# Fused attention and 4-bit FFN on eight cores: softmax scaling moved from VectorE to GpSimd, odd score blocks copied out of PSUM by VectorE

## What is computed

```python
def _mhsa(X, ln_g, ln_b, Wq, bq, Wk, bk, Wv, bv, Wo, bo):
    Xn = (X - mu) * rsqrt(var + EPS) * ln_g + ln_b
    Q, K, V = split_heads(Xn @ Wq + bq), ...         # 16 heads of 128
    scores = einsum('bhqd,bhkd->bhqk', Q, K) / sqrt(128)
    scores = where(causal, scores, -inf)
    A = softmax(scores, axis=-1)
    AV = einsum('bhqk,bhkd->bhqd', A, V)
    return AV @ Wo + bo

x = layernorm(x + attention(x))
# FFN: gate, up (16384 x 2048) and down (2048 x 16384), 4-bit values
# with one scale per 32, dequantised on the chip
x = layernorm(x + (gelu(x @ Wg.T) * (x @ Wu.T)) @ Wd.T)
```

## Time and profile before

| what | us |
|---|---|
| the kernel before, median of 2 runs | 12190.67 |
| lowest and highest of them | 11885.47, 12495.87 |
| the profiled execution, its own time | 11891.69 |
| its span, slowest core (core 7) | 11890.1 |
| spans of the eight cores | 11810.8 to 11890.1 |
| busy in the span: PE, DVE, ACT, POOL | 7283.3, 3800.4, 2362.9, 952.1 |

### The profile page before, as it was taken

The page is one execution under the profiler, slowest core; times in us unless marked ns, Lnnn a source line. Parts: engine busy times, 40 slices in busy tenths (PEclk is TensorE's granted clock), DMA queues, the critical chain, the costliest instruction groups (busy, mean ns, idle before and its releaser), DMA issues.

```text
span 11890.1 us, 99736 instructions; the slowest of 8 cores (11810.8 to 11890.1 us)
## 1 busy us (share of the span) xinstructions
PE 7283.3 (61%) x31488; PEld 3182.4 (27%) x31488; DVE 3800.4 (32%) x8321; ACT 2362.9 (20%) x3461; POOL 952.1 (8%) x1531
## 2 busy tenths in 40 slices
PE   3473341332232233777777777777756999999993
PEld 1131120111111011333233332332322444444441
DVE  1103221221221212555555555555541111221122
ACT  1213323232222112222222222222221000000001
POOL 0010000000000000111111111111100000000000
PEclk9785565556556566888888888888878999999996
DMA  5572333224324236666666666666642222222222
GB/s 82 78 91 46 48 53 65 42 45 63 47 38 61 39 36 108 115 115 111 111 111 112 113 116 112 113 111 110 111 93 92 73 76 78 75 78 71 82 72 74
DMA packets 1927393, 971.47 MB, mean 82 GB/s; under 512 B 1762928, under 2 KB 1832656, under 8 KB 1885920
## 3 DMA queue, kind: packets, MB, share of 16 engines
q0 software_dynamic: 530400, 415.45, 22.1%
q1 hardware_dynamic: 1396480, 549.66, 21.0%
HBM read 667.01 MB, written 218.10 MB: 74 GB/s over the span
## 4 chain that ended last, share of the span: by engine, by line
PE 46%; DMA 23%; DVE 13%; ACT 9%; issue 6%; SPq 2%; DVEq 0%; POOL 0%; ACTq 0%; POOLq 0%
PE pp L793 24%; PE pp L842 12%; DMA regC<-regD 8%; DMA regC<-regC 3%; PE pp L386 3%; DMA regC<-usc 3%; DVE regD L664 3%; DMA regD<-regD 3%; PE pp L288 2%; ACT regD L638 2%; PE pp L425 2%; DVE regD L497 2%; DMA regD<-wo 2%; DMA wspd<-regD 2%; PE pp L544 2%
## 5 line engine op out<-in xcount | busy, mean ns | idle before, releaser
L793 PE MATMUL pp<-regB,regC 128*128 128x512 bf16 x16384 | 3705.9, 390 | 978.8 <-ACT regC L810 603.7
L793 PEld LDWEIGHTS pp<-regB,regC 128*128 128x128 bf16 x16384 | 1635.5, 100 | 3044.3 <-issue 1215.2
L842 PE MATMUL pp<-regC,regD 128*128 128x512 bf16 x8192 | 1986.7, 406 | 528.0 <-DMA wspd<-regD 373.1
L842 PEld LDWEIGHTS pp<-regC,regD 128*128 128x128 bf16 x8192 | 833.2, 103 | 1681.4 <-issue 871.9
L425 PE MATMUL pp<-regC,regB 128*128 128x128 bf16 x2176 | 272.7, 307 | 1622.2 <-DMA regC<-regD 829.4
L815 DVE TENSOR_TENSOR regC<-regC,pp 128x512 bf16<-128x512 bf16 x512 | 328.4, 683 | 2553.7 <-PE pp L793 2553.1
L664 DVE TENSOR_TENSOR regD<-regD,regC 128x512 bf16<-128x512 bf16 (+1 forms) x1024 | 948.7, 957 | 196.2 <-ACT regD L638 179.8
L872 DVE TENSOR_TENSOR regA<-pp,regA 128x512 f32<-128x512 f32 x960 | 658.6, 690 | 1062.0 <-PE pp L842 1061.7
L638 ACT ACTIVATE regD<-regD 128x1024 bf16<-128x1024 fp8e4 (+1 forms) x512 | 432.0, 844 | 2619.2 <-DVE regD L634 2496.9
L810 ACT ACTIVATE regC<-pp 128x512 bf16<-128x512 f32 x512 | 276.6, 592 | 3063.2 <-PE pp L793 3063.2
L386 PE MATMUL pp<-regC,regD 128*128 128x512 bf16 x1024 | 351.2, 518 | 671.3 <-DVE regC L363 671.3
(11 more groups left out here) (81 smaller groups left out, 4123.9 us busy)
## 6 DMA issues: line engine op xcount, KB each, us to landing
wspg<-regC SPq DMA_DIRECT2D x128, 1024.0 KB, 4.6
regC<-wspg POOLq DMA_DIRECT2D x128, 1024.0 KB, 5.3
wspd<-regD SPq DMA_DIRECT2D x128, 512.0 KB, 3.1
regD<-wspd POOLq DMA_DIRECT2D x128, 512.0 KB, 3.9
regD<-x POOLq DMA_DIRECT2D x48, 1024.0 KB, 7.6
regD<-wq POOLq DMA_DIRECT2D x64, 512.0 KB, 6.5
regD<-wo POOLq DMA_DIRECT2D x64, 512.0 KB, 7.0
regD<-wv POOLq DMA_DIRECT2D x32, 512.0 KB, 8.0
```

What stands on the lines that cost most here:

```text
L793: e.matmul(out=pp[b][:], lhsT=WGT[:, w, k, p:256:2], rhs=H1T[:, k, tt * 1024 + t * 512: tt * 1024 + (t + 1) * 512], start=(k == 0), stop=( ...
L842: b=db, w=wd: e.matmul(out=pp[b][:], lhsT=WDT[:, p, 4 * w + c, p2:256:2], rhs=INTER[:, 2 * c + p, t * 512: (t + 1) * 512], start=(c == 0 a ...
```

## The change

Two edits, and the bookkeeping for a semaphore that POOL's computing instructions count up.

1. In `emit_tail` the scaling of the row by the reciprocal (line 408) is issued on POOL and not on DVE. It keeps its place in the Python code, so it goes into POOL's list where that list stands at the time. The transpose waits for POOL.
2. For full key blocks with odd `ks` (below the diagonal block), DVE and not ACT copies and scales the 512 scores from PSUM, followed at once by their maximum. Such a block exists once per tile in groups 3 and 2 (`ks` = 1), and not in groups 1 and 0.

```diff
-SEMS = ENGS[:3] + DMASEMS
+SEMS = ENGS[:3] + ("pool",) + DMASEMS
...
-                        ev_an = E("dve", lambda e, kl=klen_, ar=ar_, pa=par_:
+                        ev_an = E("pool", lambda e, kl=klen_, ar=ar_,
+                                  pa=par_:
                             e.tensor_scalar(
                                 out=ar[:, 0:kl], in0=ar[:, 0:kl],
                                 scalar1=stat(S_RCP + 4 * pa), scalar2=None,
...
-                            waits=mw({"dve": ev_an}, ev_atb_free[par_]),
+                            waits=mw({"pool": ev_an}, ev_atb_free[par_]),
...
                             if ks < g:
+                                if ks % 2 == 1:
+                                    eve = E("dve", lambda e, b=sb, k=ks,
+                                            ww=w, sr=srow: e.tensor_scalar(
+                                            out=sr[:, k * 512:k * 512 + ww],
+                                            in0=pp[b][:, 0:ww],
+                                            scalar1=ISQ, scalar2=None,
+                                            op0=OP.mult),
+                                        waits=mw({"pe": evs},
+                                                 ev_srow_free[par]))
+                                    ev_psum_free[sb] = {"dve": eve}
+                                    ev_cm = E("dve", lambda e, k=ks, ww=w,
+                                              sr=srow: e.tensor_reduce(
+                                            out=stat(S_CM0 + k),
+                                            in_=sr[:, k * 512:k * 512 + ww],
+                                            axis=AX, op=OP.max),
+                                        waits={"dve": eve})
+                                    ev_last_S = evs
+                                    continue
...
-        CSEMS = ("pe", "act", "dve")
+        CSEMS = ("pe", "act", "dve", "pool")
```

## The result

The changed kernel takes 13430.16 us (median of 12 runs, lowest 12878.88), the kernel before 12380.54 (median of 10, lowest 11885.47). In many executions of every kernel here the cores of one die or both ran at a lower clock and took longer: over the executions without that the ratio is 1.084, 95% interval 1.066 to 1.102, and where an experiment had few or none of them (e1, e2, e4, e6, e11) it is compared by cores 4 to 7 or by the heads of core 7 alone. The changed kernel is slower, as forecast, but by more: I had 12515 us with 12210 to 12950 for an execution like the profiled one, 5.2% over it.

The account below looks back on a forecast made before the run. The prediction took a serial ring of waits through the engines, none near full, as the bound. It added 340 + 51 + 133 + 15 + 86 = 625 us to 11891.7, forecasting 12515 us, range 12210 to 12950.

Parts of the forecast that it names:

- The ring: Per tile: DVE scaling, transpose, PE matmuls, ACT copy, DVE maxima run serially, 10.91 us a turn; additions paid in full, 256 times.
- POOL's time per scaling: Edit 1: POOL takes 1.83 us per row against DVE's 0.50, extra 1.33 us x 256 = 340 us.
- that row: DVE's line 573, the nearest plain operation: 2292 ns for 2048 columns, 1.12 ns a column, 1.22 us for the mean row.
- the sum of 625: Whole program: 340 scaling + 51 delay + 133 Wq panels + 15 Wo + 86 edit 2, in us.
- My bounds, 0 and 1150 us: POOL's scaling: from DVE's 0.50 us, extra 0, to ACT's slowest 4.59 ns a column, extra 4.49 us per row.
- POOL's delay: Edit 1: POOL reacts later to a semaphore, between 0 and 0.46 us; taken as 0.2 us x 256 = 51 us.
- The late panels: Wq panels now behind tile 2's scaling land late in every group, net 133 us; first Wo panels add about 15.
- the 193: Projections of heads 1 to 15 wait for late Wq panels, mean 3.2 us x 60 = 193 us.
- the 60 that come back: Tile 3's transposes no longer meet the panel: 3 us in group 0, 1 in group 1, x 15 = 60 back.
- Wo's 15: Two first Wo panels also stand behind the last scaling: 4 us on each of four groups, about 15.
- Edit 2: DVE's score copy lengthens tiles by 0.60 us in group 3, 0.74 in group 2: 86 us, between 45 and 105.
- much slower: Rival: POOL's scaling takes three times line 573, 3.66 us, extra 809 us, time 12985 us; chance 0.20.

Follow-up runs that it names:

- e1: Changed kernel without edit 2 (scaling on POOL, odd score block left on ACT): lowest of 6 runs 13135.68 us; heads 856 us above the kernel before.
- e2: Kernel before with edit 2 alone (DVE copies the odd score block): lowest of 6 runs 12353.70 us; heads 88 us more than before.
- e4: Kernel before, each Wq panel also waiting for tile 2's scaling of the head before, on DVE: lowest of 6 runs 12482.89 us; heads 182 us more.
- e6: Edit 1 alone, row scaled as float32 pairs by immediate 1.0, half the columns, division left out: one run, 13001.07 us; heads 3016.1 us.
- e11: As e4, but the panel waits for tile 2's reciprocal instead of its scaling: lowest of 3 runs 12664.81 us; heads 2732.5 us.
- e5: Edit 1 alone with immediate 1.0 in place of the reciprocal from memory, division left out: lowest of 3 runs 12750.87 us; heads 3368.8 us.
- e3: Changed kernel with Wq and first two Wo panels issued early, as their buffers free: lowest of 4 runs 12697.76 us; heads 234 us less than changed.
- e8: Kernel before with reciprocal, scaling (on POOL) and transpose issued behind the tile's own exponential, panels early: lowest 11312.32 us; heads 1951.3 us.

## Why the prediction missed

**Which kind of bound: right.** The ring was the right reading: a chain through five engines, none near full, in which an added microsecond is paid in full. e2 and e6 each return their own instructions' difference (88 us for 128 copies of 0.68; 353 for 352.7), and e1 returns POOL's with the late panels' added.

**POOL's time per scaling: the step that failed.** The prediction says "I take one and a half times that row, 1.83 us". It is 3.02 us, 2.5 ns a column plus 0.28, two and a quarter times line 573's 1.12 ns a column. Extra: 772.5 - 128.8 = 644 us against 340, which is 304 of the 362 us that the sum of 625 fell short of 987. My bounds, 0 and 1150 us, held it; the value was chosen by the nearest row, and that row was DVE's. A row of one engine prices another engine only as a bound. The Trainium skill's sentence that one-input operations on GpSimd are roughly at line rate (GPSIMD Engine Reference, Engine selection) is not what e1, e5 and e6 measure: 2.5 ns a column there, against VectorE's 1.12 for a plain row. The two-input ratio of 1.96 from the same page (Performance versus the Vector engine) would have been nearer, with 2.39 us, and still short.

**POOL's delay: too high.** 51 us taken, 2 measured. From the reciprocal's end to the scaling's start it is 0.17 us on POOL where it was 0.12 on DVE, 15 us in all, and from the scaling's end to the transpose's issue 0.08 where it was 0.13, 13 us back. The 0.46 us in the earlier trace rows come with issuing a DMA on POOL and not with computing there: in e4, released by the same scaling on DVE, SP's transpose starts 0.13 us after it and POOL's panel 0.66.

**The late panels: right in kind and in the number of heads, short in size, and seen in another place.** I had 193 less 60, and 15 for Wo, 148 in all. In the changed kernel the times from issue to PE of all transposes grow by 205 us and projections wait 28, 233 in all; e3, which takes the cause away, returns 234. Term by term: for the 193 stand 219 us at tile 2's transposes and 28 at the projections, 247; for the 60 that come back 37; and for Wo's 15 it is 17. I expected 190 us of projections waiting for Wq; they wait 28, because the last packets of tile 2's transpose move among the panel's and PE waits for them first. That "the panel will have landed before" tile 3's transpose was right: in group 0 it takes 2.80 us to PE where it took 4.54.

**Edit 2: right.** 86 us forecast, 88 alone (e2, 79 of them in groups 3 and 2), 110 as the difference between the changed kernel and e1.

Taken together: 644 + 2 + 233 + 88 = 967 against the heads' 966, closer than the parts are known. The sum of 625 was short by 304 for the scaling and 85 for the panels and too high by 49 for the delay. The ratio's interval lies above my 1.052 and the median of all runs above my range; 12878.88 lies inside it. The rival "much slower" (12985) was nearer than the forecast in its total, by luck: its 3.66 us for POOL and its 51 us of delay were too high, and its panels too low.

## What to carry to other kernels

Before moving work to a less busy engine, ask whether the instruction stands in the chain that sets the time: if it does, the engine's speed on that instruction is all that counts, and its idle time is worth nothing. When work joins an engine that issues DMAs, read its list again: each load behind the new instruction is issued when that instruction's inputs are ready, no longer when its buffer is free. And where no engine is full, look first at the order in which the lists are written: in this kernel another order was worth 905 us of heads without moving a single instruction to another engine.

## What was not expected of the hardware

GpSimd's multiplication of a row by a scalar takes 2.5 ns a column for bf16 and for float32 alike (2048 bf16 columns 5.43 us, 1024 float32 columns 2.77 us), with 0.28 us fixed when the scalar comes from memory and 0.20 with an immediate. DVE's same operation takes 0.72 us for 1920 bf16 columns, and DVE working beside it doesn't slow GpSimd's from 256 columns up (e8).

A transpose issued 0.14 to 0.35 us behind a 512 KB load took 9.6 and 8.6 us to PE where 4.3 is usual, though in the changed kernel over nine tenths of its packets moved before the load's first; its last ones end with the load's. One issued 0.47 us ahead of the load took 6.9 in the same place, and the narrower rows of groups 2 to 0 then lost only 0.03 to 0.15 us.
